# Attention stage of a fused attention and convolution kernel: another order of the per-tile steps on five engines

## The chip, the cores and the metric

The kernel runs on one core of a Trainium2 chip. The metric is the device time of one execution in microseconds; the number compared is the median over several runs. Everything is fp32. The core has five engines with a queue of their own each: TensorE (PE, with weight loads shown as PEld), VectorE (DVE), ScalarE (ACT), GpSimd (POOL) and SyncE (SP, which here only issues DMAs). Within one queue instructions run in the order in which they are written; between queues only semaphores order them.

## The reference

The input x has shape (8, 64, 64, 64). Two layers follow each other:

```python
# layer 0, attention over the batch axis, for each of the 4096 pixels by itself
xn = group_norm(x, 8 groups)
t  = (conv1x1(xn, ciw) + cib) as tokens (b, hw, c) + pe[:b]
tn = ln(t, ln1g, ln1b)
q, k, v = two linear maps each of tn          # 8 heads of 8 channels
scores = einsum('inhd,jnhd->nhij', q2, k2) / sqrt(8)   # i, j run over the batch of 8
z = einsum('nhij,jnhd->inhd', softmax(scores), v2) @ wout.T + bout
t = z + t
m = (ln(t, ln2g, ln2b) @ w1.T + b1) * gelu(t @ w2.T + b2) @ w3.T + b3
out = conv1x1(m + t, cow) + cob + x
# layer 1, three times, then a relu
x = x + (conv3x3(relu(conv3x3(x, w1) + b1), w2) + b2) / 3
```

## The kernel before

There are three stages in a row. `setup_weights` transposes and multiplies weights and takes the statistics of the group norm (some 44 us). `attention_block` computes layer 0 (to about 607 us). `conv_steps` computes layer 1 (the rest) and is not touched.

The attention stage works on 32 tiles of 128 pixels. One tile takes about forty steps, each a small Python function that issues the step's waits and instructions on one engine. The steps of a tile, in the order in which data flows:

- `pe_t` (L541): 1x1 convolution into PSUM; `act_t` (L666): its copy with bias to the ring buffer tt.
- `pe_qkv` twice (L553, g = 0 and 1); `act_squares` twice (L676), `act_raw` twice (L683); `dve_var1` (L733); `pool_rstd1` (L842), a power -0.5 of 8 elements on GpSimd; `act_scale` (L691), 8 activations; `pool_bias` (L738), an add of 128x1024 elements on GpSimd, SBUF to SBUF.
- `dve_p1` four times (L522, 128x1024, SBUF to SBUF, the products of q and k); `pe_scores_t` four times (L564, 8 transposes that add up in PSUM); `act_scores_t` (L696); `pe_scores` (L573); `dve_max` (L748), `dve_shift` (L759), `act_exp` (L700), `dve_sum` (L765), `dve_reciprocal` (L771), `dve_attn` (L777).
- `dve_p2` four times (L532, 128x1024, the products of attention and v); `pe_av` four times (L583); `act_z` (L705); `pe_z1` (L593); `dve_z1` (L791); `pe_center` (L603); `pe_g` (L612); `act_centered`, `act_square2` (L715, L710); `act_gelu` twice (L721).
- `pe_var2` (L619); `dve_var2` (L797); `pool_rstd2` (L847), again 8 elements; `act_rrep` (L726); `pe_rstd2` (L626); `dve_tn2` (L803); `pe_a` (L635); `dve_gated` twice (L815); `pe_out` twice (L649); `pe_cow` (L655); `dve_x` twice (L837, d = 0 and 1).

The stage is a software pipeline that is written out in full. In iteration t, each engine's `*_iteration` function issues its steps for several tiles: t, t-1, t-2 and so on. The order inside these functions and the tile offset of each step are the whole schedule. `run` calls them for t = 0 to 35 (32 tiles and 5 pipeline stages). PE issues its own list, ACT another, and so on; an engine may run ahead of another as far as the semaphores allow. Buffers: qkv and tt are rings of 4 tiles, z1, xa and xr of 2, all others single. PSUM is in full use, so that many waits are for a bank to be free.

Two waits matter below. `pe_av` for b = 0 starts to write the bank from which `dve_var2` of the tile before reads:

```python
            if b == 0:
                wait(pe, var2_done, t)
            wait(pe, p2_dve, DUOS * t + b + 1)
```

and `dve_p1` needs the finished bias of its own tile: `wait(dve, biased, t + 1)`.

Of the kernel before, what the change touches and what calls it, by code (L numbers as in the profile page):

```python
# [419 lines left out]
def attention_block(nc, d, top):  # L420


    with ExitStack() as ctx:
# [110 lines left out]
        def pe_t(pe, t, k):  # L534

            wait_loaded(pe, xa_in, t, k)
            wait(pe, raw_out[1], t)
            for j in range(2):
                for e in range(2):
                    for d in range(2):  # L540
                        m = pe.matmul(q_ps[half(d), e, 0, TILE * j:TILE * (j + 1)], top["resT"][half(e), 2 * d + j, half(e)],  # L541
                                      xa[k % 2][half(e), 2 * d + j, :], start=True, stop=True)
            m.then_inc(t_mm, 1)

        def pe_qkv(pe, t, k, g):
            wait(pe, t_out, t + 1)
            if g == 0:
                wait(pe, t_out, t + 1)
            else:
                wait(pe, raw_out[0], t + 1)  # L550
            for p in range(2):
                for d in range(2):
                    m = pe.matmul(q_ps[:, d, p, :], tt[k][half(d), TILE * (2 * g + p):TILE * (2 * g + p + 1)],  # L553
                                  top["basis"][half(d), :], start=True, stop=True)
            m.then_inc(qkv_mm[g], 1)
# [12 lines left out]
        def pe_scores(pe, t):  # L568

            wait(pe, scoresT_out, t + 1)  # L570
            wait(pe, gelu_out[1], t - 1)
            for blk in range(4):
                m = pe.transpose(b3[:, P * blk:P * (blk + 1)], scoresT[:, blk, :], ident)  # L573
            m.then_inc(scores_mm, 1)

        def pe_av(pe, t, b):
# [4 lines that stand above are left out]
            for j in (2 * b, 2 * b + 1):  # L581
                for p in range(PAIRS):
                    m = pe.matmul(b4[:, TILE * p:TILE * (p + 1)], prod2[:, j, P * p:P * (p + 1)], ident,  # L583
                                  start=(j == 0 and p == 0), stop=(j == B - 1 and p == PAIRS - 1), is_transpose=True)
            m.then_inc(av_mm, 1)

        def pe_z1(pe, t):
            wait(pe, z_out, t + 1)
            wait(pe, shift_done, upto(t + 2))
            wait(pe, gelu_out[0], t)  # L590
            for e in range(2):
                for d in range(2):
                    m = pe.matmul(zb[half(d), e, 0:HALF], top["woutT"][half(e), half(e)],  # L593
                                  z[half(e), HALF * d:HALF * (d + 1)], start=True, stop=True)
            m.then_inc(z1_mm, 1)
# [26 lines left out]
        def pe_rstd2(pe, t):  # L622
            wait(pe, rrep_done, t + 1)
            wait(pe, scoresT_out, upto(t + 3))
            for p in range(PAIRS):
                m = pe.transpose(b2[:, TILE * p:TILE * (p + 1)],  # L626
                                 rrep[:, 2 * p:2 * p + 2, :].rearrange("p a b -> p (a b)"), ident)
            m.then_inc(rstd2_mm, 1)

        def pe_a(pe, t):  # L630
            wait(pe, tn2_done, t + 1)
            wait(pe, x_done[0], t)
            wait(pe, x_done[1], t)
            for e in range(2):
                pe.matmul((b5, b7)[e][:, :], top["w1T"][half(e), :], tn2[half(e), :], start=True, stop=True).then_inc(a_mm, 1)  # L635
# [223 lines left out]


        def pe_iteration(pe, t, k, tiles):
            if tiles[0]:
                pe_t(pe, t, k)
            if tiles[2]:
                pe_scores_t(pe, t - 2, 3)
            if tiles[3]:
                pe_av(pe, t - 3, 0)
                pe_av(pe, t - 3, 1)
            if tiles[2]:
                pe_scores(pe, t - 2)  # L870
            if tiles[3]:
                pe_av(pe, t - 3, 2)
            if tiles[4]:
                pe_rstd2(pe, t - 4)
            if tiles[3]:
                pe_av(pe, t - 3, 3)
            if tiles[0]:
                pe_qkv(pe, t, k, 0)
            if tiles[3]:
                pe_z1(pe, t - 3)  # L880
            if tiles[4]:
                pe_a(pe, t - 4)
            if tiles[3]:
                pe_center(pe, t - 3, (k - 3) % RING)
            if tiles[0]:
                pe_qkv(pe, t, k, 1)
            if tiles[3]:
                pe_g(pe, t - 3, (k - 3) % RING)
            if tiles[4]:
                pe_out(pe, t - 4, 0)  # L890
                pe_out(pe, t - 4, 1)
            if tiles[1]:
                pe_scores_t(pe, t - 1, 0)
                pe_scores_t(pe, t - 1, 1)
            if tiles[3]:
                pe_var2(pe, t - 3)
            if tiles[1]:
                pe_scores_t(pe, t - 1, 2)
            if tiles[4]:
                pe_cow(pe, t - 4, (k - 4) % RING)  # L900

        def act_iteration(act, t, k, tiles):
            if tiles[1]:
                act_squares(act, t - 1, 0)
                act_raw(act, t - 1, (k - 1) % RING, 0)
            if tiles[3]:
                act_exp(act, t - 3)
            if tiles[4]:
                act_centered(act, t - 4)
                act_square2(act, t - 4)  # L910
            if tiles[1]:
                act_squares(act, t - 1, 1)
            if tiles[4]:
                act_gelu(act, t - 4, 1)
            if tiles[1]:
                act_raw(act, t - 1, (k - 1) % RING, 1)
                act_scale(act, t - 1, (k - 1) % RING)
            if tiles[2]:
                act_scores_t(act, t - 2)
            if tiles[4]:  # L920
                act_rrep(act, t - 4)
            if tiles[0]:
                act_t(act, t, k)
            if tiles[4]:
                act_gelu(act, t - 4, 0)
            if tiles[3]:
                act_z(act, t - 3)

        def dve_iteration(dve, t, k, tiles):
            if tiles[1]:  # L930
                dve_p1(dve, t - 1, (k - 1) % RING, 1)
            if tiles[4]:
                dve_gated(dve, t - 4, 1)
                dve_gated(dve, t - 4, 0)
            if tiles[1]:
                dve_p1(dve, t - 1, (k - 1) % RING, 2)
            if tiles[2]:
                dve_sum(dve, t - 2)
            if tiles[0]:
                dve_var1(dve, t)  # L940
            if tiles[1]:
                dve_p1(dve, t - 1, (k - 1) % RING, 3)
            if tiles[2]:
                dve_reciprocal(dve, t - 2)
                dve_attn(dve, t - 2)
                dve_p2(dve, t - 2, (k - 2) % RING, 0)
            if tiles[3]:
                dve_var2(dve, t - 3)
            if tiles[2]:
                dve_p2(dve, t - 2, (k - 2) % RING, 1)  # L950
                dve_p2(dve, t - 2, (k - 2) % RING, 2)
            if tiles[4]:
                dve_x(dve, t - 4, (k - 4) % RING, 1)
            if tiles[2]:
                dve_p2(dve, t - 2, (k - 2) % RING, 3)
            if tiles[1]:
                dve_max(dve, t - 1)
                dve_shift(dve, t - 1)
            if tiles[4]:
                dve_x(dve, t - 4, (k - 4) % RING, 0)  # L960
            if tiles[3]:
                dve_tn2(dve, t - 3)
            if tiles[0]:
                dve_p1(dve, t, k, 0)
            if tiles[2]:
                dve_z1(dve, t - 2, (k - 2) % RING)

        def pool_iteration(pool, t, k, tiles):
            if tiles[4]:
                pool_rstd2(pool, t - 4)  # L970
            if tiles[1]:
                pool_bias(pool, t - 1, (k - 1) % RING)
            if tiles[0]:
                pool_rstd1(pool, t)

        def sp_iteration(sp, t, k, tiles):
            if 2 <= t + 1 < TILES:
                sp_xa(sp, t + 1, k + 1)
            if tiles[4]:
                sp_xr(sp, t - 4, k - 4)  # L980

        def run(eng, iteration):

            for t in range(TILES + 5 - 1):
                iteration(eng, t, t % RING, [0 <= t - s < TILES for s in range(5)])

        block = ctx.enter_context(nc.Block())

# [448 lines left out]
```

## Time and profile before

| what | value |
|---|---|
| median of 3 runs | 1165.74 us (1165.06 to 1167.67) |
| profiled execution: its time, its span | 1166.12 us, 1164.30 us |
| mean granted TensorE clock | 0.987 of full speed |
| PE busy | 1078.2 us, 93% of the span |
| DVE busy | 1060.3 us, 91% |
| ACT busy | 653.4 us, 56% |
| POOL busy | 525.9 us, 45% |

The span is the time from the first to the last instruction of the profiled execution; 1.82 us lie around it. A busy share of 1 on two engines at once says that each had an instruction in flight all the time. It does not yet say which of the two sets the pace.

```profile
PE   3279999999999999999969999999999999999995
DVE  5459999999999999999958999999999999999995
ACT  4558888888888888988613232332234232342332
POOL 5134555444554555545323444534435445444440
PEclk9989999999999999999989999999999999999998
```

Each digit is the busy share of a fortieth of the span (29 us) in tenths. Digits 2 to 20 are the attention stage, the rest is the convolution.

### The profile page before, as it was taken

The numbers are of one execution on the slowest core, as the hardware profiler recorded it, in microseconds if no ns is written. First come the engines' busy times: TensorE is split into PE (matmuls) and PEld (weight loads), VectorE is DVE, ScalarE is ACT, GpSimd is POOL, SyncE is SP. The second block draws the span as 40 slices with busy tenths as digits, with TensorE's granted clock in tenths as the row PEclk, the third lists the DMA queues.
The fourth block names the chain that finished last, engine by engine and source line by source line (L and its number), as shares of the span: only waits on it lengthen the run. The fifth ranks groups of instructions, "written<-read, shape, count | busy, mean of one in ns | idle before, by whom it ended". The sixth has DMA issues, their size and how long they took to land. (4 is left out here: it accounts for less than half of the span.)

```text
span 1164.3 us, 20990 instructions
## 1 busy us (share of the span) xinstructions
PE 1078.2 (93%) x7238; PEld 604.7 (52%) x7238; DVE 1060.3 (91%) x1481; ACT 653.4 (56%) x1525; POOL 525.9 (45%) x416
## 2 busy tenths in 40 slices
PE   3279999999999999999969999999999999999995
PEld 3167777777777777777633333333333333333331
DVE  5459999999999999999958999999999999999995
ACT  4558888888888888988613232332234232342332
POOL 5134555444554555545323444534435445444440
PEclk9989999999999999999989999999999999999998
DMA  8101111111111111110000000210003000120003
GB/s 304 53 20 28 37 38 29 38 29 37 35 32 29 37 37 33 34 28 20 20 10 1 1 1 1 46 28 1 1 1 73 1 1 1 29 45 1 1 1 73
DMA packets 87544, 35.83 MB, mean 31 GB/s; under 512 B 70209, under 2 KB 86850, under 8 KB 86930
## 3 DMA queue, kind: packets, MB, share of 16 engines
q1 hardware_dynamic: 85634, 33.81, 11.0%
q8 instruction: 61, 1.00, 0.4%
q0 software_dynamic: 768, 0.33, 0.1%
q10 hardware_dynamic: 1040, 0.35, 0.1%
q14 instruction: 41, 0.34, 0.1%
HBM read 26.09 MB, written 8.39 MB: 30 GB/s over the span
## 5 line engine op out<-in xcount | busy, mean ns | idle before, releaser
L1082 PE MATMUL acc<-mixed,cwp 128*128 128x512 f32 x768 | 354.4, 607 | 5.1 <-DVE mixed L1143 2.9
L1082 PEld LDWEIGHTS acc<-mixed,cwp 128*128 128x128 f32 x768 | 139.7, 191 | 218.6 <-issue 214.8
L1100 ACT ACTIVATE y<-acc,cols 128x1024 f32<-128x1024 f32 x96 | 111.6, 1207 | 249.4 <-PE acc L1092 249.4
L1092 PE MATMUL acc<-mixed,cwp 64*64 64x512 f32 x1536 | 184.2, 600 | 11.7 <-POOL mixed L1143 11.5
L842 POOL TENSOR_TENSOR rstd<-var,half 128x8 f32<-128x8 f32 x32 | 80.9, 2527 | 217.6 <-DVE var L733 217.6
L522 DVE TENSOR_TENSOR prod<-qkv 128x1024 f32<-128x1024 f32 x128 | 155.6, 1219 | 7.6 <-POOL qkv L738 7.3
L532 DVE TENSOR_TENSOR prod<-attn,qkv 128x1024 f32<-128x1024 f32 x128 | 155.0, 1235 | 1.1
L1142 POOL TENSOR_TENSOR mixed<-xs 128x256 f32<-128x256 f32 x92 | 83.1, 903 | 156.7 <-DVE xs L1131 156.7
L564 PE MATMUL cb<-consts,prod 128*128 128x128 f32 x1024 | 135.8, 283 | 0.0
L1108 DVE TENSOR_TENSOR y<-y,acc 128x512 f32<-128x512 f32 x192 | 120.5, 678 | 15.9 <-ACT y L1100 15.9
L1116 DVE TENSOR_TENSOR y<-y,acc 128x512 f32<-128x512 f32 x192 | 123.0, 682 | 7.2 <-PE acc L1092 5.2
L583 PE MATMUL cb<-consts,prod 128*128 128x128 f32 x1024 | 127.9, 273 | 1.6 <-DVE prod L532 0.9
L564 PEld LDWEIGHTS cb<-consts,prod 128*128 128x128 f32 x1024 | 117.0, 147 | 19.1 <-issue 17.7
L1092 PEld LDWEIGHTS acc<-mixed,cwp 64*64 64x64 f32 x1536 | 50.5, 132 | 135.8 <-issue 102.8
L583 PEld LDWEIGHTS cb<-consts,prod 128*128 128x128 f32 x1024 | 114.7, 141 | 2.8 <-DVE prod L532 1.7
L1123 ACT ACTIVATE h<-y 128x512 f32<-128x512 f32 x96 | 56.5, 624 | 98.4 <-DVE y L1116 98.0
L738 POOL TENSOR_TENSOR qkv<-qkv,brep 128x1024 f32<-128x1024 f32 x32 | 106.3, 3321 | 9.0 <-ACT qkv L691 9.0
L847 POOL TENSOR_TENSOR rstd<-var,half 128x8 f32<-128x8 f32 x32 | 80.6, 2519 | 61.6 <-DVE var L797 61.6
L1142 POOL TENSOR_TENSOR mixed<-h 128x256 f32<-128x256 f32 x48 | 47.8, 996 | 129.6 <-ACT h L1123 129.6
L691 ACT ACTIVATE qkv<-qkv,rstd 128x192 f32<-128x192 f32 x256 | 92.1, 442 | 13.3 <-POOL rstd L842 13.2
L1136 DVE TENSOR_TENSOR mixed<-xs 128x512 f32<-128x512 f32 x96 | 94.1, 1029 | 0.4
L553 PE MATMUL q_ps<-basis,tt 64*128 64x256 f32 x512 | 77.3, 423 | 11.3 <-ACT tt L666 5.9
(172 smaller groups left out, 1550.1 us busy)
## 6 DMA issues: line engine op xcount, KB each, us to landing
xs<-in_x SPq DMA_DIRECT2D x4, 2048.0 KB, 16.6
xa<-in_x SPq DMA_DIRECT2D x32, 256.0 KB, 2.8
xr<-in_x SPq DMA_DIRECT2D x64, 128.0 KB, 2.9
out_y<-xs SPq DMA_DIRECT2D x32, 256.0 KB, 4.7
cw<-in_L_conv_w POOLq DMA_DIRECT2D x2, 144.0 KB, 4.2
consts<-in_consts ACTq DMA_DIRECT2D x1, 192.0 KB
group<-in_consts SPq DMA_DIRECT2D x1, 64.0 KB
w1n<-in_L_conv_w ACTq DMA_DIRECT2D x1, 64.0 KB
```

What stands on the lines that cost most here:

```text
L522: return eng.tensor_tensor(out, q, kk, ALU.mult)
L532: return eng.tensor_tensor(out, a, v, ALU.mult)
L564: m = pe.matmul(b2[:, P * b:P * (b + 1)], prod1[:, e, P * b:P * (b + 1)], ident, start=(e == 0), stop=(e == HD - 1), is_transpose=True)
L583: m = pe.matmul(b4[:, TILE * p:TILE * (p + 1)], prod2[:, j, P * p:P * (p + 1)], ident, start=(j == 0 and p == 0), stop=(j == B - 1 and p = ...
L738: pool.tensor_tensor(qk, qk, top["brep"][:, :].unsqueeze(1).broadcast_to([P, B, 2 * C]), ALU.add).then_inc(biased, 1)
L1082: pe.matmul(psum[PSUM_PAIR[v, q, j]][i][:, :, :], weights(v, i, j).rearrange("p n o -> p (n o)"), mixed[v][i][:, s0:s0 + WIDE, j, :], star ...
L1092: m = pe.matmul(psum[PSUM_PAIR[v, q, j]][i][out, :, :], edge_weights(v, i, j)[rows, :], mixed[v][i][rows, s0 + near:s0 + near + WIDE, j, : ...
L1100: act.activation(pairs(y[i][q][:, :, :]), m1, ACT.Identity, bias=cols[:, (6, 8)[v]:(7, 9)[v]]).then_inc(m1_out[i][q], 1)
L1108: m = dve.tensor_tensor(even_odd, even_odd, psum[PSUM_PAIR[v, q, 3]][i][:, :, :], op)
L1116: dve.tensor_tensor(even_odd, even_odd, psum[PSUM_PAIR[v, q, j]][i][:, :, :], ALU.add).then_inc(y_done[i][q][j], 1)
L1136: eng.tensor_tensor(r, pairs(x[:, :, 0:HW]), pairs(x[:, :, 2:2 + HW]), ALU.subtract).then_inc(outer_done[i][c], 1)
L1142: eng.tensor_tensor(r[:, :, 2, :], even_odd[:, 0], even_odd[:, 1], ALU.add)
```

## The change

Only the five `*_iteration` functions and the length of the loop differ; no step's instructions or waits are changed. The numbering of the tiles moves by up to two iterations (most steps of t-3 become steps of t-4 and so on; 7 stages, 38 iterations, of which the first and last hold few steps). Apart from the numbering, each engine's list is a cycle, and written as a cycle from a common point the lists differ as follows.

- PE: before `... scoresT 0, 1; var2; scoresT 2; cow; t; scoresT 3; av 0; av 1 ...`, after `... scoresT 0, 1, 2; var2; scoresT 3; av 0; t; cow; av 1 ...`.
- DVE: `p1 3` goes from ahead of `reciprocal, attn` to behind them; `x 1` from between `p2 2` and `p2 3` to behind `p2 3`; `x 0` from behind `shift` to between `max` and `shift`; `gated 1, gated 0` become `gated 0, gated 1`.
- ACT: `gelu 0` goes from behind `act_t` to directly behind `gelu 1`, ahead of `raw 1`.
- POOL: the cycle rstd1, rstd2, bias is the same.
- SP: the loads of xr are issued for tile t-5 in place of t-4, beside xa of tile t+1 as before.

```diff
         def pe_iteration(pe, t, k, tiles):
+            if tiles[6]:
+                pe_cow(pe, t - 6, (k - 6) % RING)
+            if tiles[4]:
+                pe_av(pe, t - 4, 1)
+            if tiles[3]:
+                pe_scores(pe, t - 3)
...
+            if tiles[5]:
+                pe_out(pe, t - 5, 0)
+                pe_out(pe, t - 5, 1)
+            if tiles[2]:
+                pe_scores_t(pe, t - 2, 0)
+                pe_scores_t(pe, t - 2, 1)
+                pe_scores_t(pe, t - 2, 2)
+            if tiles[4]:
+                pe_var2(pe, t - 4)
             if tiles[2]:
                 pe_scores_t(pe, t - 2, 3)
             if tiles[3]:
                 pe_av(pe, t - 3, 0)
...
+            if tiles[0]:
+                pe_t(pe, t, k)
+
+        def act_iteration(act, t, k, tiles):
             if tiles[3]:
+                act_scores_t(act, t - 3)
+            if tiles[5]:
+                act_rrep(act, t - 5)
+            if tiles[1]:
+                act_t(act, t - 1, (k - 1) % RING)
             if tiles[4]:
+                act_z(act, t - 4)
...
             if tiles[4]:
                 act_gelu(act, t - 4, 1)
+                act_gelu(act, t - 4, 0)
...
+        def dve_iteration(dve, t, k, tiles):
+            if tiles[4]:
+                dve_p2(dve, t - 4, (k - 4) % RING, 2)
+                dve_p2(dve, t - 4, (k - 4) % RING, 3)
+            if tiles[6]:
+                dve_x(dve, t - 6, (k - 6) % RING, 1)
+            if tiles[3]:
+                dve_max(dve, t - 3)
+            if tiles[6]:
+                dve_x(dve, t - 6, (k - 6) % RING, 0)
+            if tiles[3]:
+                dve_shift(dve, t - 3)
...
+            if tiles[3]:
+                dve_sum(dve, t - 3)
+            if tiles[1]:
+                dve_var1(dve, t - 1)
+            if tiles[3]:
+                dve_reciprocal(dve, t - 3)
+                dve_attn(dve, t - 3)
+            if tiles[2]:
+                dve_p1(dve, t - 2, (k - 2) % RING, 3)
+            if tiles[3]:
+                dve_p2(dve, t - 3, (k - 3) % RING, 0)
             if tiles[4]:
+                dve_var2(dve, t - 4)
             if tiles[3]:
+                dve_p2(dve, t - 3, (k - 3) % RING, 1)
...
-            for t in range(TILES + 5 - 1):
-                iteration(eng, t, t % RING, [0 <= t - s < TILES for s in range(5)])
+            for t in range(TILES + 7 - 1):
+                iteration(eng, t, t % RING, [0 <= t - s < TILES for s in range(7)])
```

## Rows read from the trace of the kernel before

**Rows 1.** Windows view: stretch, its length, busy us (instructions) of each engine, clock, DMA.

```profile
94.14:555.67 461.53, 461.53 (x4304) 350.86 (x4300) 448.99 (x596) 403.57 (x1137) 240.26 (x85) 1.00 0.13 32
555.67:607.02 51.35, 42.08 (x328) 26.81 (x324) 38.04 (x54) 21.33 (x34) 12.68 (x6) 0.93 0.07 17
```

**Rows 2.** Windows view of one iteration, the columns as in rows 1.

```profile
210.08:226.36 16.28, 16.28 (x155) 12.37 (x153) 15.84 (x22) 14.21 (x41) 7.60 (x3) 1.00 0.13 34
```

**Rows 3.** Timeline of DVE at 210 us: start, length, engine, line, operation, idle before.

```profile
210.44 1.23 DVE L522 TENSOR_TENSOR prod<-qkv 128x1024 f32<-128x1024 f32 x1 [0.29 <-issue]
```

**Rows 4.** Timeline of DVE, one iteration, 302 to 317 us.

```profile
302.81 0.75 DVE L791 SCALAR_TENSOR_TENSOR z<-zb,cols,tt 128x512 f32<-128x512 f32 x1 [0.28 <-PE zb L593]
...
307.07 0.68 DVE L765 TENSOR_REDUCE den<-shifted 128x64 f32<-128x512 f32 x1
307.66 0.17 DVE L733 TENSOR_SCALAR var<-sumsq 128x8 f32<-128x8 f32 x1
307.76 1.23 DVE L522 TENSOR_TENSOR prod<-qkv 128x1024 f32<-128x1024 f32 x1
308.91 0.55 DVE L771 RECIPROCAL rden<-den 128x64 f32<-128x64 f32 x1
309.49 0.69 DVE L777 TENSOR_TENSOR attn<-shifted,rden 128x512 f32<-128x512 f32 x1
310.21 1.23 DVE L532 TENSOR_TENSOR prod<-attn,qkv 128x1024 f32<-128x1024 f32 x1
311.36 0.16 DVE L797 TENSOR_SCALAR var<-cb 128x8 f32<-128x8 f32 x1
...
315.24 0.68 DVE L748 TENSOR_REDUCE smax<-zb 128x64 f32<-128x512 f32 x1
316.01 0.69 DVE L759 TENSOR_TENSOR shifted<-zb,smax 128x512 f32<-128x512 f32 x1
316.62 0.47 DVE L837 SCALAR_TENSOR_TENSOR xs<-b,cols,xr 128x256 f32<-128x256 f32 x1
```

**Rows 5.** Timeline of PE, the same iteration, 307 to 315 us.

```profile
307.27 1.97 PE L564 MATMUL cb<-consts,prod 128*128 128x128 f32 x16
309.07 0.95 PE L619 MATMUL cb<-consts,sq 128*128 128x2 f32 x8
...
310.88 0.66 PE L655 MATMUL b<-z,cowT 64*64 64x256 f32 x8
311.36 0.62 PE L541 MATMUL q_ps<-xa,resT 64*64 64x128 f32 x16
311.91 1.09 PE L564 MATMUL cb<-consts,prod 128*128 128x128 f32 x8
312.84 1.91 PE L583 MATMUL cb<-consts,prod 128*128 128x128 f32 x16
314.59 0.60 PE L573 MATMUL zb<-consts,scoresT 128*128 128x128 f32 x4
```

**Rows 6.** Timeline of DVE and PE in the ramp: a product held up, its reader.

```profile
86.49 3.38 DVE L532 TENSOR_TENSOR prod<-attn,qkv 128x1024 f32<-128x1024 f32 x1
...
89.92 0.77 PE L583 MATMUL cb<-consts,prod 128*128 128x128 f32 x5 [0.92 <-DVE prod L532]
```

**Rows 7.** Timeline of ACT, the same iteration as rows 4.

```profile
309.47 0.81 ACT L683 ACTIVATE qkv<-q_ps 128x768 f32<-128x768 f32 x1
...
313.31 0.57 ACT L696 ACTIVATE scoresT<-cb 128x512 f32<-128x512 f32 x1
```

**Rows 8.** Timeline of POOL: a power step alone, then both in the steady state.

```profile
54.36 1.64 POOL L842 TENSOR_TENSOR rstd<-var,half 128x8 f32<-128x8 f32 x1 [12.40 <-DVE var L733]
...
307.91 2.59 POOL L842 TENSOR_TENSOR rstd<-var,half 128x8 f32<-128x8 f32 x1 [6.65 <-DVE var L733]
311.60 2.55 POOL L847 TENSOR_TENSOR rstd<-var,half 128x8 f32<-128x8 f32 x1 [1.10 <-DVE var L797]
```

**Rows 9.** Timeline of PE in the drain of the pipeline.

```profile
561.82 0.66 PE L593 MATMUL zb<-z,woutT 64*64 64x256 f32 x8 [0.69 <-ACT z L705]
```

More of the change, by code:

```diff
@@ L861, in pe_iteration @@
         def pe_iteration(pe, t, k, tiles):
-            if tiles[0]:
-                pe_t(pe, t, k)
+            if tiles[6]:
[5 more added lines that the diff above has]
+            if tiles[4]:
+                pe_av(pe, t - 4, 2)
+            if tiles[5]:
+                pe_rstd2(pe, t - 5)
+            if tiles[4]:
+                pe_av(pe, t - 4, 3)
+            if tiles[1]:
+                pe_qkv(pe, t - 1, (k - 1) % RING, 0)
+            if tiles[4]:
+                pe_z1(pe, t - 4)
+            if tiles[5]:
+                pe_a(pe, t - 5)
+            if tiles[4]:
+                pe_center(pe, t - 4, (k - 4) % RING)
+            if tiles[1]:
+                pe_qkv(pe, t - 1, (k - 1) % RING, 1)
+            if tiles[4]:
+                pe_g(pe, t - 4, (k - 4) % RING)
+            if tiles[5]:
+                pe_out(pe, t - 5, 0)
[4 more added lines that the diff above has]
+                pe_scores_t(pe, t - 2, 2)
+            if tiles[4]:
+                pe_var2(pe, t - 4)
             if tiles[2]:
@@ L867, in pe_iteration @@
                 pe_av(pe, t - 3, 0)
-                pe_av(pe, t - 3, 1)
-            if tiles[2]:
-                pe_scores(pe, t - 2)
+            if tiles[0]:
+                pe_t(pe, t, k)
+        def act_iteration(act, t, k, tiles):
             if tiles[3]:
-                pe_av(pe, t - 3, 2)
-            if tiles[4]:
[L874 to L902, printed above, removed]
+                act_scores_t(act, t - 3)
+            if tiles[5]:
+                act_rrep(act, t - 5)
+            if tiles[1]:
+                act_t(act, t - 1, (k - 1) % RING)
+            if tiles[4]:
+                act_z(act, t - 4)
             if tiles[1]:
@@ L917, in act_iteration @@
                 act_scale(act, t - 1, (k - 1) % RING)
+        def dve_iteration(dve, t, k, tiles):
+            if tiles[4]:
+                dve_p2(dve, t - 4, (k - 4) % RING, 2)
[8 more added lines that the diff above has]
+                dve_shift(dve, t - 3)
+            if tiles[5]:
+                dve_tn2(dve, t - 5)
@@ L918, in act_iteration @@
             if tiles[2]:
-                act_scores_t(act, t - 2)
+                dve_p1(dve, t - 2, (k - 2) % RING, 0)
             if tiles[4]:
-                act_rrep(act, t - 4)
-            if tiles[0]:
-                act_t(act, t, k)
+                dve_z1(dve, t - 4, (k - 4) % RING)
+            if tiles[2]:
+                dve_p1(dve, t - 2, (k - 2) % RING, 1)
+            if tiles[5]:
+                dve_gated(dve, t - 5, 0)
+                dve_gated(dve, t - 5, 1)
+            if tiles[2]:
+                dve_p1(dve, t - 2, (k - 2) % RING, 2)
@@ L924, in act_iteration @@
+            if tiles[3]:
+                dve_sum(dve, t - 3)
+            if tiles[1]:
+                dve_var1(dve, t - 1)
+            if tiles[3]:
+                dve_reciprocal(dve, t - 3)
+                dve_attn(dve, t - 3)
+            if tiles[2]:
+                dve_p1(dve, t - 2, (k - 2) % RING, 3)
+            if tiles[3]:
+                dve_p2(dve, t - 3, (k - 3) % RING, 0)
             if tiles[4]:
-                act_gelu(act, t - 4, 0)
+                dve_var2(dve, t - 4)
@@ L926, in act_iteration, with pool_iteration @@
             if tiles[3]:
-                act_z(act, t - 3)
-        def dve_iteration(dve, t, k, tiles):
+                dve_p2(dve, t - 3, (k - 3) % RING, 1)
+        def pool_iteration(pool, t, k, tiles):
             if tiles[1]:
[L931 to L966, printed above, removed]
@@ L968, in pool_iteration @@
-        def pool_iteration(pool, t, k, tiles):
+                pool_rstd1(pool, t - 1)
             if tiles[4]:
@@ L972, in pool_iteration @@
                 pool_bias(pool, t - 1, (k - 1) % RING)
-            if tiles[0]:
-                pool_rstd1(pool, t)
         def sp_iteration(sp, t, k, tiles):
@@ L978, in sp_iteration @@
                 sp_xa(sp, t + 1, k + 1)
-            if tiles[4]:
-                sp_xr(sp, t - 4, k - 4)
+            if tiles[5]:
+                sp_xr(sp, t - 5, k - 5)
         def run(eng, iteration):
-            for t in range(TILES + 5 - 1):
-                iteration(eng, t, t % RING, [0 <= t - s < TILES for s in range(5)])
+            for t in range(TILES + 7 - 1):
+                iteration(eng, t, t % RING, [0 <= t - s < TILES for s in range(7)])
         block = ctx.enter_context(nc.Block())
```

## The prediction

> **What bounds the kernel now.** I read the windows view by stage first. From 94.14 to 555.67 us PE is busy for all 461.53 us, DVE for 448.99 (97%), ACT for 87%, POOL for 52% [rows 1]. This is the steady state of the pipeline: one iteration takes 16.28 us, so it holds 461.53 / 16.28 = 28.3 iterations. Two engines look full, and the change is worth something only if it relieves the one that sets the pace. DVE has a wait: in each iteration the add behind the z1 matmul stands idle for 0.28 us, and the one it waits for is PE [rows 4]. The iteration at 210 us is the better witness. There DVE lost 0.29 us for no reason that the profile shows, ahead of a product [rows 3]; the iteration still took 16.28 us, with PE busy for all of it [rows 2]. So DVE had slack of about 0.3 us, and PE had none. PE sets the pace.
>
> Is PE's 16.28 us work, or does it hide waits in matmuls whose ends are modelled? The starts tell. Two blocks of scoresT take 309.07 - 307.27 = 1.80 us, two av blocks with the same count of matmuls 314.59 - 312.84 = 1.75 us [rows 5]. The 0.05 us more, and about 0.1 us of gap ahead of it, come where the shape of the matmul (128\*128, 64\*128, 64\*64, 128\*64) changes. The changes of shape are the only irregular places that I find. I take them as a cost of the order and not as waits.
>
> **The change on PE.** No matmul is added or removed, so PE's iteration can shrink only through fewer changes of shape. Around the cycle before: av (128\*128), qkv, z1, a, center, qkv with g, out, scoresT, cow with t, and back: nine changes. After: the same nine. cow and t (both 64\*64) move together from between scoresT 2 and 3 to between av 0 and av 1, both 128\*128 blocks; var2 (128\*128) moves inside its block. Before, cow and t took 0.48 + 0.55 = 1.03 us from start to next start [rows 5]. After, t and then cow take the same matmuls and the same gap in and out. Nothing shows that order, so I bound it by 0.05 us to either side per iteration, the extra of a first block after a change of shape, and take 0. Over 28.3 iterations that is 0, with 1.4 us to either side.
>
> **The change on DVE.** Three spacings show what it removes. Shift starts 0.77 us behind max, on whose result it waits, and x follows shift after 0.61 (316.62 - 316.01); attn starts 0.58 behind reciprocal; the first p2 product 0.72 behind attn [rows 4]. With x 0 between max and shift, the wait on max falls: 0.77 becomes about 0.59, as sum to var1 (307.66 - 307.07), a gain of 0.18. With p1 3 between attn and p2 0, 0.72 becomes about 0.60, a gain of 0.12. With the z1 wait of 0.28, and the 0.08 by which an instruction that need not wait starts before the product ahead of it ends (307.76 + 1.23 against 308.91), DVE could run in 16.28 - 0.66 = 15.62 us. If DVE set the pace, this would be worth 0.66 x 28.3 = 19 us. It does not, so DVE will wait more: the z1 add still starts when PE's z1 matmuls end, and the wait of 0.28 grows to about 0.28 + 0.18 + 0.12 = 0.6 us. Value in the steady state: 0, the bounds being 0 and 19 us.
>
> **What could now come late.** I lay the new lists over this iteration's clock, PE at its own pace. PE: scoresT 0, 1 from 307.27, scoresT 2 at 309.07, var2 at 309.94, scoresT 3 at 310.75, av 0 at 311.66, t at 312.63, cow at 313.1, av 1 at 313.7, scores at 314.59 as before. DVE is tied to PE at 302.81, so var1 stays at 307.66; from there reciprocal 307.78 (the sum ends at 307.75), attn 308.36, p1 3 at 308.97, p2 0 at 310.12, var2 at 311.26.
> - scoresT 3 needs p1 3, which ends at 308.97 + 1.23 = 310.20: 0.5 us early.
> - av 0 needs p2 0 (310.12 + 1.23 = 311.35) and dve_var2 (311.26 + 0.16 = 311.42). DVE to PE takes 0.05 us: the held-up product ended at 86.49 + 3.38 = 89.87, the matmul started at 89.92 [rows 6]. The weight load of av 0 goes one matmul (0.11) ahead of it, at 311.55. It has 0.08 us of slack. Before, av 0 stood 1.2 us later in the cycle and this was no concern. Everything behind av 0 on PE would wait with it, and through z1 all of DVE.
> - scores at 314.59 needs act_scores_t. gelu 0 now stands ahead of raw 1, which starts at 309.47 + 0.59 and ends at about 310.87, where scale had been ready at 310.53. So scale slips by 0.4 us, and act_scores_t from 313.31 to 313.7, ending 314.27 [rows 7]. Slack about 0.15 us with the weight load. The cover is thin but there, and ACT pays the 0.4 us out of its idle time ahead of act_z.
> - t and cow come 1.3 and 2.2 us later. qkv waits for act_t, which stays where ACT's list has it, at 314.7; x 1 starts at 314.75, after cow ends at 313.8. No cost. The xr loads go out a whole iteration ahead of use.
>
> **GpSimd.** The power step takes 1.64 us alone and 2.59 and 2.55 in the steady state [rows 8]: it stands behind a p1 or p2 product that has begun, for about 0.9 us. With reciprocal and attn behind var1, rstd1 starts beside the reciprocal and may end 0.95 us earlier; raw 1 then ends the wait of scale, not rstd1, so this is worth 0 in the steady state. The bias add is next in POOL's queue, at 314.05. p2 3 is then under way (its products follow each other every 1.14 us, so it ends at about 314.8), the bias gets through behind it and runs some 2.3 us beside x 1, max, x 0, shift and tn2, all with a PSUM input, as before; it ends near 317.1, and p1 0 wants it at 317.4. Where bias has begun and a product wants to start, the product is held: 3.38 us instead of 1.2 [rows 6], once, in the ramp. By my walk one p2 product of that iteration is still held.
>
> The Trainium skill ("SBUF — State Buffer", section "Who interferes with whom") says that a DVE instruction with two SBUF inputs and a GpSimd instruction that reads SBUF exclude each other for the whole instruction, by order of issue. By it, attn would now be held by rstd1. It is a rival below. The trace does not bear it out for the power step: rstd1 runs from 307.91 to 310.50 and attn (309.49) and p2 0 (310.21) begin within it at their plain 0.69 and 1.23 us.
>
> **Ramp and drain.** The same steps in the same dependences; the two further iterations are numbering. In the ramp I find 0.1 us (the early rstd1 moves one scale and bias ahead, then the held product takes it back). In the drain, once t and qkv are gone, PE waits (0.69 us for act_z at 561.82 [rows 9]) and DVE binds for two iterations: 0.3 us less, minus 0.1 where sum and reciprocal now touch, in each; the last p2 stands one x (0.4) earlier, and cow with its changes of shape (0.5) now lies inside the last tile's av blocks. Together about 0.5 us less; bounds 1.5 less and 1.5 more.
>
> **The sum.** 0 + 0 - 0.1 - 0.4 = -0.5 us. Against the profiled execution: 1166.12 (span 1164.30 and 1.82 around) gives 1165.6. That execution lies 0.4 above the median, so the median becomes 1165.2.
>
> **Rivals.**
> - DVE sets the pace, and PE's gaps are waits in disguise. For it: 97% busy [rows 1]. Against: [rows 2, 3]. It gives up to -19 us, 1147; if PE's real floor is only a third of the way down, -6, 1160. Chance 0.12, mostly at the mild end.
> - Slower: dve_var2 reaches PE after 311.55 and stalls av 0 in every iteration. It decides from 0.08 us on; each further 0.1 us costs 2.8. A wait behind max or sum that takes 0.1 to 0.2 longer than I read gives +1 to +4 us: 1166 to 1170. Chance 0.13 that it passes the mark.
> - attn held for the whole power step: rstd1 from 307.91 to 309.55 moves attn from 308.36 to 309.55, 1.2 us; less 0.1 of slack, 1.1 x 28.3 = +31 us, 1197. [rows 4, 8] speak against it: chance 0.02.
> - The ramp gains the whole 2.2 us of the held product, with the drain -3 us: 1163. Chance 0.06.
>
> **The numbers.** A change of 0.2% (2.3 us) is what can be told from none: below 1163.4 is faster, above 1168.1 slower. The likeliest case, no change, has 0.67; faster 0.18; slower 0.15. My forecast's own range is 1163.5 to 1167.5. Four fifths of the chance lie between 1160.5 and 1169.
>
> **What would show it.** Right: PE busy for all of the steady state again, iterations of 16.28 us, DVE idle ahead of the z1 add 0.5 to 0.6 us, rstd1 1.64 to 2.1 us long, DVE's sum unchanged. Wrong: an iteration other than 16.28; if shorter, look at PE's starts around changes of shape; if longer, at what av 0 or scores waited for, and at attn beside rstd1.

## The result, and the profile after

The changed kernel takes 1167.55 us in the median of 22 runs (1164.86 to 1170.04), the kernel before 1165.42 in 22 runs beside them: ratio 1.0017, interval 1.001 to 1.0024. It is slower, by 2.1 us or 0.2%, where 1165.2 and no change were forecast: under the 1168.1 from which the prediction calls it slower, and 0.05 us above the forecast's own range (1163.5 to 1167.5). The profiled execution took 1169.86 us, its span 1168.1. Of the experiments below, one run each of e1 (1753.20 us at a mean clock of 0.606) and of e10 (1379.79 us at 0.778) lies far outside the others of its kernel and is left out.

The steady state first, in the windows view of the kernel after (columns as in [rows 1]: the length, then busy us and instructions of PE, PEld, DVE, ACT and POOL, then the granted clock; the last two lines are two stretches of the drain):

```profile
95.65:556.82 461.17, 461.17 (x4295) 348.30 (x4294) 446.13 (x595) 399.46 (x1136) 203.39 (x85) 1.00 0.13 33
586.00:590.00 4.00, 4.00 (x26) 3.08 (x25) 3.29 (x5) 0.63 (x1) 1.73 (x1) 0.57 0.00 0
600.00:620.00 20.00, 12.85 (x32) 4.92 (x33) 12.67 (x20) 0.31 (x1) 8.57 (x14) 0.50 0.00 0
```

PE is busy for all of it, as in [rows 1], and an iteration still takes 16.28 us. One iteration of DVE (timeline; it answers to [rows 4], and its times stand 1.15 us later than there):

```profile
303.96 0.75 DVE L791 SCALAR_TENSOR_TENSOR z<-zb,cols,tt 128x512 f32<-128x512 f32 x1 [0.46 <-PE zb L593]
...
308.93 0.55 DVE L771 RECIPROCAL rden<-den 128x64 f32<-128x64 f32 x1
309.51 0.69 DVE L777 TENSOR_TENSOR attn<-shifted,rden 128x512 f32<-128x512 f32 x1
310.12 1.22 DVE L522 TENSOR_TENSOR prod<-qkv 128x1024 f32<-128x1024 f32 x1
311.26 1.22 DVE L532 TENSOR_TENSOR prod<-attn,qkv 128x1024 f32<-128x1024 f32 x1
312.39 0.16 DVE L797 TENSOR_SCALAR var<-cb 128x8 f32<-128x8 f32 x1
312.47 3.49 DVE L532 TENSOR_TENSOR prod<-attn,qkv 128x1024 f32<-128x1024 f32 x3
315.88 0.47 DVE L837 SCALAR_TENSOR_TENSOR xs<-b,cols,xr 128x256 f32<-128x256 f32 x1
316.37 0.69 DVE L748 TENSOR_REDUCE smax<-zb 128x64 f32<-128x512 f32 x1
316.98 0.48 DVE L837 SCALAR_TENSOR_TENSOR xs<-b,cols,xr 128x256 f32<-128x256 f32 x1
```

POOL in the same iteration, which answers to [rows 8]:

```profile
309.06 1.65 POOL L842 TENSOR_TENSOR rstd<-var,half 128x8 f32<-128x8 f32 x1 [7.13 <-DVE var L733]
312.63 2.55 POOL L847 TENSOR_TENSOR rstd<-var,half 128x8 f32<-128x8 f32 x1 [1.93 <-DVE var L797]
315.15 3.04 POOL L738 TENSOR_TENSOR qkv<-qkv,brep 128x1024 f32<-128x1024 f32 x1
```

and PE, which answers to [rows 5]:

```profile
312.81 1.04 PE L583 MATMUL cb<-consts,prod 128*128 128x128 f32 x8
313.77 0.67 PE L541 MATMUL q_ps<-xa,resT 64*64 64x128 f32 x16
314.26 0.61 PE L655 MATMUL b<-z,cowT 64*64 64x256 f32 x8
314.80 1.09 PE L583 MATMUL cb<-consts,prod 128*128 128x128 f32 x8
315.73 0.60 PE L573 MATMUL zb<-consts,scoresT 128*128 128x128 f32 x4
```

Take 1.15 us off and the walk of the prediction is there: av 0 at 311.66 (forecast 311.66), t at 312.62 (312.63), cow at 313.11 (313.1), scores at 314.58 (314.59); DVE's var2 at 311.24 (311.26). DVE waits 0.46 us for z1, not 0.28, and nothing came of the DVE time saved.

So the 2.1 us lie outside the steady state. I cut the two traces at the same matmuls of PE (us):

| stretch | before | after | difference |
|---|---|---|---|
| first matmul of the attention stage (44.59 in both) to z1 of tile 3 | 94.69 | 95.65 | +0.96 |
| to z1 of tile 28 (25 iterations) | 407.00 | 407.19 | +0.19 |
| to z1 of tile 31 | 43.35 | 44.93 | +1.57 |
| to the last cow | 14.95 | 15.48 | +0.53 |
| to the first edge matmul of the convolution | 15.76 | 16.22 | +0.46 |
| to the end | 543.96 | 544.00 | +0.04 |

These sum to 3.75 us, where the two profiled executions differ by 3.74 (1169.86 - 1166.12). The drain in PE's timeline of the kernel after:

```profile
585.17 1.08 PE L583 MATMUL cb<-consts,prod 128*128 128x128 f32 x8 [1.10 <-DVE var L797]
586.18 1.13 PE L655 MATMUL b<-z,cowT 64*64 64x256 f32 x8
587.24 3.12 PE L583 MATMUL cb<-consts,prod 128*128 128x128 f32 x16
590.20 0.60 PE L626 MATMUL cb<-consts,rrep 128*128 128x128 f32 x4
```

and of the kernel before:

```profile
582.86 0.66 PE L655 MATMUL b<-z,cowT 64*64 64x256 f32 x8
584.07 3.35 PE L583 MATMUL cb<-consts,prod 128*128 128x128 f32 x24 [0.55 <-DVE var L797]
```

Before, cow ran while PE waited for dve_var2 of the last tile. After, PE waits 1.10 us with nothing to do, and cow stands between the av blocks, on the path. Then something that the walk did not have: the 16 matmuls of av 1 and 2 take 2.96 us from start to next start (590.20 - 587.24), where 16 of them take 1.75 in [rows 5]. The records have the granted clock at half, 1.2 instead of 2.4 GHz, from 586.2 to 589.6 us, so cow and most of the 16 matmuls behind it ran at half clock. Windows of the kernel before for the same stretches:

```profile
586.00:590.00 4.00, 3.27 (x31) 2.39 (x29) 2.79 (x5) 1.80 (x3) 0.63 (x1) 1.00 0.04 10
600.00:620.00 20.00, 13.34 (x36) 4.74 (x32) 13.25 (x20) 0.00 (x0) 8.58 (x14) 0.68 0.00 0
```

The clock was 1.00 there before and 0.57 after; from 600 to 620, where the last tile runs alone, 0.68 and 0.50. In both traces it is at half again from about 1156 us to the end, when no matmul is left to run. In the ramp the records have half clock from 76.9 to 83.7 before and from 74.2 to 84.5 after; PE's qkv block there (timeline, before and after):

```profile
74.44 1.14 PE L553 MATMUL q_ps<-basis,tt 64*128 64x256 f32 x8 [0.45 <-ACT tt L666]
```
```profile
74.43 2.08 PE L553 MATMUL q_ps<-basis,tt 64*128 64x256 f32 x8 [0.45 <-ACT tt L666]
```

The same eight matmuls, started at the same time: the clock alone makes them 0.94 us longer, and that is nearly the whole 0.96 of the first stretch.

Ahead of the first clock record (70.1 us before, 67.4 after) the windows view prints 1.00, but there is no record behind it. The matmuls there take as long as at half clock: the same block of eight at 63.95 us in the kernel before, and in e9, where the records are at full clock:

```profile
63.95 2.08 PE L553 MATMUL q_ps<-basis,tt 64*128 64x256 f32 x8 [1.81 <-ACT qkv L683]
```
```profile
61.71 1.14 PE L575 MATMUL q_ps<-basis,tt 64*128 64x256 f32 x8 [0.27 <-ACT qkv L719]
```

### The profile page after: what moved, and what is told of

It reads as the page before. It is cut to its first block and busy times, and to the rows that moved or that the text cites. A ratio compares the mean times of both kernels' runs of the same rounds, so it can differ in the third digit from the quotient of the medians.

```text
span 1168.1 us, 20990 instructions
## 1 busy us (share of the span) xinstructions
PE 1080.9 (93%) x7238; PEld 603.5 (52%) x7238; DVE 1057.8 (91%) x1481; ACT 650.0 (56%) x1525; POOL 488.5 (42%) x416
## 5 line engine op out<-in xcount | busy, mean ns | idle before, releaser
L532 DVE TENSOR_TENSOR prod<-attn,qkv 128x1024 f32<-128x1024 f32 x128 | 152.5, 1234 | 0.0
L842 POOL TENSOR_TENSOR rstd<-var,half 128x8 f32<-128x8 f32 x32 | 53.6, 1676 | 232.5 <-DVE var L733 232.5
L847 POOL TENSOR_TENSOR rstd<-var,half 128x8 f32<-128x8 f32 x32 | 80.6, 2520 | 86.8 <-DVE var L797 86.8
L738 POOL TENSOR_TENSOR qkv<-qkv,brep 128x1024 f32<-128x1024 f32 x32 | 96.1, 3004 | 9.0 <-ACT qkv L691 9.0
```

The lines of the kernel that those rows point to most:

```text
L532: return eng.tensor_tensor(out, a, v, ALU.mult)
L738: pool.tensor_tensor(qk, qk, top["brep"][:, :].unsqueeze(1).broadcast_to([P, B, 2 * C]), ALU.add).then_inc(biased, 1)
```

## The experiments

Twelve runs of kernels, each beside the kernel before on the same chip.

**Which engine's list is it?** The new order of PE alone, then the new orders of DVE and ACT alone. The edit is the list itself: e1 is the kernel before with pe_iteration of the change (and the renumbered lists of POOL and SP, whose cycles are the same), e2 the changed kernel with pe_iteration of before. The whole function is written anew in e1; the steps of PE that change places, put side by side, each with the tile numbers of its own kernel:

```
             if tiles[2]:
                 pe_scores_t(pe, t - 2, 0)
                 pe_scores_t(pe, t - 2, 1)
+                pe_scores_t(pe, t - 2, 2)
             if tiles[4]:
                 pe_var2(pe, t - 4)
-                pe_scores_t(pe, t - 1, 2)
-                pe_cow(pe, t - 4, (k - 4) % RING)
+            if tiles[2]:
+                pe_scores_t(pe, t - 2, 3)
+            if tiles[3]:
+                pe_av(pe, t - 3, 0)
+            if tiles[0]:
+                pe_t(pe, t, k)
```

> Only PE's list is the new one; ACT and DVE keep the order of before. Theory (PE pace, loss by clock outside the steady state): iterations of 16.28 us; the drain has the new idle stretch of PE ahead of the last tile's first av block and cow inside its av blocks; the time is that of the changed kernel, about 1167 us (+1 to +3 over before). Rival (the loss is in ACT's or DVE's list, or in waits of the steady state): as before, 1165.4, or iterations longer than 16.28.

> The new ACT and DVE lists with PE's list of before. Theory: iterations of 16.28 us, the PE idle stretch ahead of the last tile's first av block is about 0.6 us as before, the time is that of before, 1165.4 (-1 to +0.7). Rival (ACT or DVE): 1167 or more.

e1 took 1215.56 to 1216.78 us in four runs, ratio 1.0435 (1.0421 to 1.0449), a time that neither theory had. A second profile was to show why:

> A second look at the kernel with PE's new list alone (ACT's and DVE's of before), which took 1216 us and whose only trace ran at a granted clock of 0.55. What this one is to tell: which wait adds the 1.8 us per iteration. By my walk none should: x 1 waits 0.07 us for cow, var2 reaches PE 0.02 us late. If DVE's x 1 ahead of p2 3 is what stalls, DVE is idle ahead of L837 and PE ahead of an av block; if the bias is (its power steps and the bias beside other products than in either kernel), a product of 128x1024 takes 3.4 us instead of 1.2 in each iteration.

1218.16 us, with iterations of 18.11 us. DVE, POOL and PE of it, in order of engine (timelines):

```profile
318.59 3.33 DVE L532 TENSOR_TENSOR prod<-attn,qkv 128x1024 f32<-128x1024 f32 x1
...
318.47 2.37 POOL L738 TENSOR_TENSOR qkv<-qkv,brep 128x1024 f32<-128x1024 f32 x1
...
321.98 1.10 PE L583 MATMUL cb<-consts,prod 128*128 128x128 f32 x8 [1.15 <-DVE prod L532]
```

The same two instructions in the kernel before (timelines of DVE and POOL):

```profile
314.11 1.21 DVE L532 TENSOR_TENSOR prod<-attn,qkv 128x1024 f32<-128x1024 f32 x1
```
```profile
314.11 3.43 POOL L738 TENSOR_TENSOR qkv<-qkv,brep 128x1024 f32<-128x1024 f32 x1
```

There they start together, and it is the add that waits. With PE's cow later, x 1 starts 0.12 us later behind the products ahead of it (2.40 us behind the start of p2 1 instead of 2.28), and the last p2 product starts 0.12 us after the GpSimd bias add has begun. It is held until the add ends: 3.33 us instead of 1.22, in every iteration, and PE waits 1.15 us for it. In the changed kernel x 1 stands behind that product. So the product starts first, the bias add (315.15, 3.04 us) goes through behind it, and neither costs PE anything. The Trainium skill ("SBUF — State Buffer", section "Who interferes with whom") has a rule for a DVE instruction with two SBUF inputs and a GpSimd instruction that reads SBUF: the one issued first excludes the other for its whole instruction. This trace agrees for the bias add, with 2.1 us of hold. For the power step the changed kernel shows nothing of the kind: attn and p1 3 start inside rstd1 and take their plain 0.69 and 1.22 us.

e2 took 1168.19 us (11 runs), 1.002 (1.0011 to 1.0029), where 1165.4 was expected: a miss, and the rival (the loss lies with the lists of ACT or DVE, 1167 or more) is what came. PE's old order does not bring the time back. Its 25 steady iterations take 407.00 us, as before; its profile loses 0.61 us in the ramp, with a half clock from 89.7 to 93.1, and 1.2 us behind z1 of tile 31, with one from 598.3 to 618.8.

**Is it cow's place in the drain?** The changed kernel, with cow ahead of av 0 in the last iterations, where it fills PE's wait, and nothing else.

```
-            if tiles[6]:
+            if tiles[6] and t - 1 <= TILES + 1:
...
+            if t > TILES + 1 and 0 <= t - 5 < TILES:
+                pe_cow(pe, t - 5, (k - 5) % RING)
```

> The changed kernel; only in its last four iterations cow stands ahead of av 0, as before. Nothing of the steady state moves. Theory: the last tile's av blocks run at full clock again, drain 1 to 1.7 us shorter than in the changed kernel's trace, time 1165.5 to 1166.3 (the ramp's part stays). Rival (ramp or steady state): no change, 1167.5.

1166.46 us (11 runs), 1.0005 (0.9996 to 1.0014): 0.16 us above the range expected; of the 2.1 us it leaves a remainder that can't be told from none. PE and the windows in its trace:

```profile
582.81 0.66 PE L655 MATMUL b<-z,cowT 64*64 64x256 f32 x8
583.98 3.35 PE L583 MATMUL cb<-consts,prod 128*128 128x128 f32 x24 [0.51 <-DVE var L797]
```
```profile
586.00:590.00 4.00, 3.27 (x30) 2.36 (x28) 2.69 (x5) 1.23 (x2) 0.53 (x1) 1.00 0.09 22
600.00:620.00 20.00, 14.00 (x34) 4.86 (x31) 13.25 (x20) 0.00 (x0) 8.58 (x14) 0.55 0.00 0
```

The clock is 1.00 again at 586 us, and from z1 of tile 28 to z1 of tile 31 it takes 43.22 us, 1.71 less than the changed kernel and 0.13 less than before. The tail is still at 0.55. Its drain has cow where e2 has it, and yet it is 1.7 us faster than e2; no run tells why.

**Is it the clock?** Matmuls on constants go where PE stands idle in the drain, in both kernels. Nothing else changes, and they write PSUM that nothing reads at the time.

```
+        def fill(pe, n):
+            wait(pe, raw_out[1], TILES)
+            for _ in range(n):
+                pe.matmul(q_ps[:, 0, 0, 0:P], ident, ident, start=True, stop=True)
...
+            if t >= TILES - 3:
+                fill(pe, 2)
...
+            if t == TILES - 1:
+                fill(pe, 8)
```

> The changed kernel with extra matmuls on TensorE, whose results nobody reads, in its idle stretches from the last three tiles to the start of the convolution (8 ahead of the last av 0, 5 ahead of each of the last three z1, 16 ahead of the last rstd2, 5 ahead of its a, 12 ahead of its out, 10 behind its cow, 12 and 14 at the start of the convolution). Theory (clock): no stretch of granted 0.5 between 580 and 622 us, 4 to 6 us less than the changed kernel, 1162 to 1163.5, and a smaller spread. Rival (the order itself costs, not the clock): the extra matmuls only cost, 1167.5 or more.

> The kernel before with extra matmuls in TensorE's idle stretches from the last three tiles to the start of the convolution, half as many as in the first filled kernel, whose trace showed each to cost two passes of 0.11 us, so that they overfilled the gaps. Theory (clock): no stretch of granted 0.5 from 590 to 620 us, and 2 to 4 us less: 1161.5 to 1163.5. Rival (clock not what costs there): 1165.4 or more.

> The changed kernel with the same fillers (4 instead of 2 ahead of the last av 0, where its idle stretch is 1.1 instead of 0.55 us). Theory (the loss of the change is clock in the drain, and a different share of it from run to run): within 0.6 us of the filled kernel before. Rival (the order of the drain itself costs): 1.5 to 2 us above the filled kernel before.

e4 took 1169.27 us, 1.0032 (1.002 to 1.0045): a miss of size. The clock was full (0.995), but each filler was two passes of 0.11 us and I had counted one, so they ran over the gaps and delayed the work. With half as many (two more in the changed kernel, ahead of its longer wait): the kernel before 1162.19 us (6 runs), 0.9968 (0.9957 to 0.998), the changed one 1161.27 (5 runs), 0.9969 (0.9956 to 0.9981). The medians are 0.92 us apart where 0.6 was expected, in favour of the changed kernel; the ratios are the same, and the runs overlap (1161.04 to 1162.90, 1161.21 to 1163.28). With the clock up in the drain the 2.1 us are gone, and both beat the kernel before. The changed kernel filled (e8):

```profile
586.00:590.00 4.00, 3.76 (x36) 2.93 (x34) 2.44 (x5) 1.11 (x2) 0.00 (x0) 1.00 0.23 53
600.00:620.00 20.00, 18.31 (x107) 9.92 (x106) 14.66 (x24) 2.32 (x2) 8.59 (x14) 1.00 0.00 1
```

Its three stretches behind z1 of tile 28 are 43.30, 13.18 and 13.58 us, those of before filled 43.35, 13.13 and 13.58. Without fillers the last two had been 14.95 and 15.76 in the kernel before: the low clock cost it 4 us there as well.

The same in the ramp (gaps of the statistics stage and of tiles 0 to 2):

> The filled kernel before, with extra matmuls also in TensorE's idle stretches from 28 to 78 us (22 and 4 in the weight stage, 1 to 14 ahead of the first qkv, t and scores steps). Theory (matmuls of the ramp run at half speed, 2.08 instead of 1.13 us for a qkv step): no stretch of 0.5 before the end, each of the first qkv steps 0.95 us shorter, 3 to 6 us less than the filled kernel: 1156.5 to 1159.5. Rival (fillers overshoot while the clock is low): 1162 or more.

> The same fillers in the changed kernel. Theory: within 0.7 us of the filled kernel before with fillers in the ramp, since with a full clock nothing tells the two orders apart. Rival (the orders differ in themselves): more than 1 us apart.

1158.97 us (5 runs), 0.9941 (0.9929 to 0.9953), and 1159.03 (5 runs), 0.994 (0.9927 to 0.9953). These are the fastest kernels of the study that compute all of it. A half clock is left from about 41 to 48 and from 72 to 75 us; the first record of full clock comes at 34 us, where it came at 67 to 70 without the fillers of the ramp.

**Does the low clock fall by chance?** A second profile of the changed kernel, to see whether the half clock lies elsewhere.

> A second profile of the changed kernel. Theory: iterations of 16.28 us again, while the stretches of granted 0.5 before 84 us and from 586 to 620 us lie elsewhere or have other lengths; the difference of its span from the first profile's (1168.1) is theirs. Rival: the same stretches at the same places, a fixed cost.

1169.55 us, with half clock from 74.1 to 84.3, 586.1 to 589.5 and 599.7 to 620.2 us: the same places within 0.2 us, as the rival had it. The runs without a trace list only a mean clock, and the time goes with it: the changed kernel's five runs at 0.988 average 1165.6 us, eight at 0.985 1167.3, seven at 0.980 to 0.982 1169.5. Of the kernel before, 47 runs beside the experiments list it: 12 at 0.988 average 1165.2 us (1164.4 to 1166.5), seven at 0.985 1166.6, and none lies under 0.983. So most of the difference is how often an execution keeps the clock, and how long; at an equal mean clock 0.4 to 0.7 us remain, which no run explains.

**What is the new order worth where PE has room?** Both kernels with one of the four var2 matmuls per tile; the variances of the other token pairs are left out, and the output is not that of the reference.

```
-            for p in range(PAIRS):
-                m = pe.matmul(b4[:, 2 * p:2 * p + 2], sq2[:, TILE * p:TILE * (p + 1)], cmean[:, ::C], start=True, stop=True)
+            m = pe.matmul(b4[:, 0:2 * PAIRS], sq2[:, 0:TILE], cmean[:, ::C // 4], start=True, stop=True)
```

> The kernel before, with one of the four matmuls of var2 per tile (the variances of the other token pairs are left out): 0.67 us less of TensorE per iteration. Theory (PE sets the pace at 16.28, DVE follows at 15.9): iterations of 15.9 us, 10 us less in all, 1155. Rival (DVE or a wait sets the pace already): unchanged, 1165.

> The changed kernel with the same matmuls left out. By the DVE list alone it could go to 15.65. But the loop from PE's z1 over DVE's z1 add, sums, p1 3, p2 0 and var2 back to av 0 took 9.4 us, and from av 0 to the next z1 PE needs 6.7: I expect this loop to bind at 16.1 to 16.2 us, 2 to 4 us less than the changed kernel, so SLOWER than the light kernel before. Rival (the new order has the slack that its DVE list suggests): 15.65, 1150.

The order before: 1155.09 us, 0.9908 (0.9892 to 0.9923). The new order: 1162.88 us, 0.9972 (0.9961 to 0.9983). The edit takes 0.67 us per iteration from PE (var2's block took 0.81 us up to the next start and takes 0.14). The order before goes down to 15.88 us and DVE's limit: from 150 to 500 us DVE waits for nothing. The new one goes only to 16.13. One iteration of e6 (windows view), then what PE's weight loads ahead of av waited for in e7 (waits view, 150 to 500 us: total us, times, longest us) and two successive av 0 blocks of e7 (timeline):

```profile
300.00:315.88 15.88, 15.84 (x148) 11.69 (x146) 15.72 (x23) 14.21 (x41) 8.50 (x3) 1.00 0.14 35
```
```profile
PEld cb L583 <- DVE var L796: 7.4, 21, 0.4
```
```profile
310.92 1.08 PE L583 MATMUL cb<-consts,prod 128*128 128x128 f32 x8
...
327.06 1.08 PE L583 MATMUL cb<-consts,prod 128*128 128x128 f32 x8
```

The weight load of av 0 waits for dve_var2 in each of 21 iterations, 0.35 us in the mean, and av 0 starts 1.23 us behind scoresT 3 (310.92 - 309.69), where it is 0.91 in the changed kernel. Av 0 earlier in the cycle closes a loop, z1 on PE, then DVE's list from the z1 add to dve_var2, then av 0 and the rest of PE up to z1, that takes 16.13 us by itself. At 16.28 it is hidden by 0.15. So the better DVE order has no better floor: it moved the limit from DVE to this loop.

## Why the prediction was wrong

**What bounds the kernel: right.** PE sets the pace. The DVE time saved was worth nothing, and DVE's z1 wait grew, to 0.46 us instead of the 0.5 to 0.6 that I walked. The spacings that I priced came: max, x 0 and shift take 0.17 less together, and the product behind attn starts after 0.61 instead of 0.72. The missing 0.1 us is at a step that I had not priced: max starts 0.49 behind x 1 (315.88 to 316.37), where shift starts 0.39 behind x 0.

**PE's shape changes: right.** Zero per iteration, with a bound of 0.05 either way; the iteration is 16.28 us.

**The slack of av 0: right, and real.** A product had slipped by 0.29 us in the kernel before and cost nothing [rows 2, 3]. The same slip, now of the reciprocal, in the kernel after (timeline of DVE, then the waits view, 95 to 555 us):

```profile
211.39 0.55 DVE L771 RECIPROCAL rden<-den 128x64 f32<-128x64 f32 x1 [0.28 <-issue]
```
```profile
DVE z L791 <- PE zb L593: 13.1, 28, 0.7
PEld cb L583 <- DVE var L797: 0.2, 1, 0.2
```

The weight load of av 0 waited once, 0.2 us, for dve_var2, and that fits the +0.19 of 25 iterations. The rival that it stalls in each iteration did not come, but e7 shows the loop that it named, 0.15 us below the pace, where the walk had 0.08.

**GpSimd: right for this change.** rstd1 is alone now, 1.65 us long, attn is not held, the bias add hurts nobody in the steady state. The rival that attn is held was wrong. What I did not see is that this depends on x 1 standing behind the last p2 product (e1): for PE's list alone I expected 1 to 3 us, and it cost 50.

**The drain: this step failed.** "Together about 0.5 us less", and -0.4 in the sum; measured +1.57 to z1 of tile 31 and +0.99 from there to the convolution. Two things were wrong with it. The first is the gain. It was to come in the iterations up to tile 30, and the two intervals of z1 there sum to 31.27 us both before and after. With the clock held up, the three stretches behind z1 of tile 28 sum to 70.06 us in both orders (e5, e8): the order is worth 0 there.

The second is the clock, and it made the loss. All the prices in the sum were rows at full clock; that cow had filled PE's wait before, and what becomes of PE when nothing does, I had not asked. For cow inside the av blocks I counted 0.5 us. It took 1.06 (587.24 - 586.18), all of it at half clock, and the 16 matmuls behind it 1.21 us more than in [rows 5]. The same steps of the last tile in e8, in the same order at full clock:

```profile
584.30 0.66 PE L671 MATMUL b<-z,cowT 64*64 64x256 f32 x8
584.89 1.97 PE L591 MATMUL cb<-consts,prod 128*128 128x128 f32 x16
586.69 0.60 PE L638 MATMUL cb<-consts,rrep 128*128 128x128 f32 x4
```

There cow takes 0.59 and the 16 matmuls 1.80 us, and from av 0 to z1 it is 5.56 us (583.29 to 588.85), as it is 5.57 in the kernel before (584.07 to 589.64) without cow in between. e3, which moves only cow, takes 1.71 us out of this stretch of the changed kernel.

**The ramp: this term failed too.** Forecast -0.1, measured +0.96 in the profiled run. The dependences are as walked. The half clock came 2.7 us earlier and left 0.8 later. That the new order causes this is not shown: e3 and e8 have the same ramp lists as the changed kernel, and e3 took 94.71 us to z1 of tile 3, with half clock from 75.2 to 82.0, e8 93.75, with none recorded there. With the lists of before it was 94.69, and 95.06 in e5.

That the clock carries most of the loss is shown by e5 and e8: with it held up in the drain, 1162.19 and 1161.27 us, and by e9 and e10 within 0.1. None of the rivals had this cause. That 1167.55 misses the forecast's own range by only 0.05 us, and lies within the four fifths (1160.5 to 1169), is owed to widths given for other reasons.

**Open.** e2 has PE's old order and full pace in the steady state, and yet lies at 1.002. Its tail had the long half clock of the changed kernel. Why DVE's and ACT's new order leads to that with PE's matmuls where they were, no run tells, and e2 was not run with fillers. Nor do I know how the 2.1 us of the medians split between ramp and drain; the split above is that of one execution, and the second profile repeats it.

## What to carry to other kernels

When an order of work is changed, read the fill and the drain apart from the loop, and price matmuls there at the clock that the records grant, not at that of the loop: work moved out of a gap may cost the clock of the blocks behind it. In a loop that one engine paces, an order that saves time on another is worth nothing by itself; ask with a lightened kernel whether it lowers the next floor or adds a loop of waits just under the present one. Lists of several engines that were found together are to be tried together: here PE's alone cost 4%.

## What the runs showed of the hardware

- Half clock came in ramp and drain, and behind the last matmul, where PE had stood idle for parts of the time before, and not in 461 us of full work. In the kernel before it cost about 4 us in the last tile and the start of the convolution (14.95 + 15.76 against 13.13 + 13.58 us). Some 40 filler matmuls in the drain gave 0.3%, and some 70 in the ramp 0.3% more, with no change in the work that counts.
- Two profiles of one program have their half clock at the same places within 0.2 us, and still single runs go from 1164.9 to 1170.0 with a mean clock from 0.988 to 0.980.
- An fp32 matmul of 128x128 on constants takes two passes of 0.11 us.
- A GpSimd add of 128x1024 holds a product of two SBUF operands that starts 0.12 us behind it for 2.1 us. Where the product is 0.4 us ahead, the add waits some 0.7 instead (3.04 us against 2.37), and the product is not delayed.
